# An attention output projection with its bias as a product on TensorE, row stores on GpSimd, and another order on SyncE and at the entry

## The reference

```python
x = x + attention(layernorm(x), ctx, ctx)        # ... @ Wo + bo
h = layernorm(x)
logits = h @ W_router.T + b_router               # 8 experts
w, idx = top_k(softmax(logits), 2)
x = x + sum(w * (h @ W_experts[idx].T + b_experts[idx]))
```

## Time and profile before

| | us |
|---|---|
| median of 3 runs | 2529.03 (2528.85 to 2530.27) |
| profiled execution, its own time | 2535.11 |
| its span | 2533.0 |

### The profile page before, as it was taken

How to read it: one execution, slowest core, us unless ns; L and a number is a source line. 1 busy time by engine, 2 the same in 40 slices (tenths; PEclk the granted TensorE clock), 3 DMA queues, 4 the chain that set the end, 5 groups by cost and what they waited for, 6 DMA issues and landing times. The chain is left out here.

```text
span 2533.0 us, 37104 instructions
## 1 busy us (share of the span) xinstructions
PE 2423.8 (96%) x13490; PEld 1286.3 (51%) x13490; DVE 2181.5 (86%) x1941; ACT 1836.9 (73%) x2150; POOL 424.0 (17%) x514
## 2 busy tenths in 40 slices
PE   8999779999999999999999999999999999869998
PEld 7878424444444444444444444444444447658776
DVE  4368569999999999999999999999999988876565
ACT  3123469999999998999999999999999854423343
POOL 2113200000000000000000000000000014336664
PEclk9999889999999999999999999999999999969999
DMA  7436781111152111115111112511111128734463
GB/s 268 155 127 219 199 202 27 26 27 30 26 121 56 27 26 31 26 30 138 36 26 31 26 27 50 126 26 31 26 26 47 31 97 307 250 108 143 133 220 118
DMA packets 145945, 230.90 MB, mean 91 GB/s; under 512 B 29126, under 2 KB 74662, under 8 KB 145004
## 3 DMA queue, kind: packets, MB, share of 16 engines
q1 hardware_dynamic: 123116, 176.93, 24.5%
q0 software_dynamic: 22016, 51.13, 6.4%
q10 hardware_dynamic: 640, 0.52, 0.1%
HBM read 154.75 MB, written 91.43 MB: 97 GB/s over the span
## 5 line engine op out<-in xcount | busy, mean ns | idle before, releaser
L1085 ACT ACTIVATE probs<-psum 128x1024 f32<-128x1024 f32 x1600 | 1513.4, 1034 | 138.5 <-PE psum L1239 131.6
L1239 PE MATMUL psum<-q_st,k_st 97*128 97x512 f32 x3200 | 923.7, 420 | 31.6 <-ACT probs L1085 18.9
L1239 PEld LDWEIGHTS psum<-q_st,k_st 97*128 97x128 f32 x3200 | 549.6, 189 | 609.5 <-ACT probs L1085 412.7
L1147 DVE TENSOR_TENSOR even_sums<-even_sums,probs 128x2048 f32<-128x2048 f32 x352 | 805.7, 2289 | 19.1 <-ACT probs L1085 19.1
L1260 PE MATMUL psum<-probs,v_st 128*32 128x512 f32 x6400 | 801.7, 602 | 0.0
L1147 DVE TENSOR_TENSOR odd_sums<-odd_sums,probs 128x2048 f32<-128x2048 f32 x320 | 731.3, 2285 | 1.0
L1260 PEld LDWEIGHTS psum<-probs,v_st 128*32 128x32 f32 x6400 | 152.5, 108 | 353.2 <-issue 273.6
L1990 PE MATMUL psum<-we_hi,wo 128*128 x624 | 218.8, 412 | 6.5 <-issue 6.2
L764 POOL DMA_DIRECT2D sum_scratch<-shared_rows x31 | 18.4, 593 | 1216.0 <-ACT shared_rows L1040 1216.0
L1847 ACT ACTIVATE wo<-psum 128x512 fp32r<-128x512 f32 x78 | 46.7, 598 | 136.5 <-PE psum L1976 115.5
L1990 PEld LDWEIGHTS psum<-we_hi,wo 128*128 128x128 f32 x624 | 119.0, 191 | 33.3 <-issue 7.7
(11 more groups left out here) (226 smaller groups left out, 2083.9 us busy)
## 6 DMA issues: line engine op xcount, KB each, us to landing
q_st<-qh_scratch SPq DMA_DIRECT2D x64, 256.0 KB
k_st<-kh_scratch SPq DMA_DIRECT2D x56, 192.0 KB, 3.8
token_rows<-rows SPq DMA_DIRECT2D x8, 1028.0 KB, 5.3
xn<-in_x SPq DMA_DIRECT2D x16, 512.0 KB, 6.7
qh_scratch<-o_hi SPq DMA_DIRECT2D x8, 1024.0 KB, 4.5
ql_scratch<-o_lo SPq DMA_DIRECT2D x8, 1024.0 KB, 7.1
q_st<-ql_scratch SPq DMA_DIRECT2D x32, 256.0 KB
token_rows<-in_x SPq DMA_DIRECT2D x1, 8192.0 KB, 36.3
```

The costliest lines, as they stand in the source:

```text
L1085: nc.scalar.activation(probs[:, p_slot(it, t), 2 * half:2 * half + 2, :], psum[:, 2 * slot:2 * slot + 2, :], ACT.Exp, scale=SCALE).then_in ...
L1147: nc.vector.tensor_tensor(into[:], a, probs[:, p_slot(it, t)], ALU.add).then_inc(added, 1)
L1239: mm = nc.tensor.matmul(psum[:, 2 * slot + h % 2, :], k_st[:, h, t * P:(t + 1) * P], q_st[:, b, h, :], start=True, stop=True)
```

## The change

The output bias is no longer added to x by GpSimd. A tensor `bo_pair` of 64 partitions holds the high part of the bias in rows 0 to 31 and the low part in rows 32 to 63 (512 columns), and beside it 128 columns that are zero but for ones in rows 0 and 32. `project_rows` begins with one product of the two, which puts the bias into psum; the 12 products add to it. The high part is copied by ScalarE and the low part computed by GpSimd during attention.

GpSimd issues `store_rows` and `store_mix` instead of SyncE. SyncE loads the attended rows at even i with the same condition on projection i + 1, ahead of the x load and the expert piece of that step, and loads x and pieces in another order at the start. At the entry ScalarE splits the first expert piece ahead of the last result; VectorE's preparation (`beside`) is spread behind the residuals of tiles 0 to 3; TensorE takes the router sums at step 2 behind project(2) instead of at step 0. One iota moves to `mix_experts`. Some small buffers are shared (`ex` with `below`, one `stats` for two).

```diff
@@ project_rows
+    bo, picks = g["bo_pair"][:, 0:g["D"]], g["bo_pair"][:, g["D"]:]
+    pe.matmul(psum[:, bank, :], picks, bo, start=True, stop=False)
     for t, (j, A, W) in enumerate(terms):
-        mm = pe.matmul(psum[:, bank, :], A[:, j, i % 2, :], W[:, j, :], start=t == 0, stop=t == len(terms) - 1)
+        mm = pe.matmul(psum[:, bank, :], A[:, j, i % 2, :], W[:, j, :], start=False, stop=t == len(terms) - 1)
@@ attention, gpsimd
+                    if it == 1:
+                        pool.wait_ge(bo_high_ready, 1)
+                        pool.tensor_tensor(bo_pair[DH:, 0:D], bo_raw[DH:, :], bo_pair[DH:, 0:D].bitcast(F32), ALU.subtract).then_inc(wo_lo_ready, 1)
@@ attention, scalar
+                        if it == 1 and n == NP // 3:
+                            act.wait_ge(small_in, 48)
+                            act.activation(bo_pair[:, 0:D], bo_raw[:], ACT.Copy).then_inc(bo_high_ready, 1)
@@ route_tokens, sync
-                for i in range(RING):
-                    load_x(i)
-                    load_piece(i)
+                load_x(0)
+                load_piece(0)
+                load_x(1)
+                load_x(2)
+                load_piece(1)
+                load_piece(2)
                 for i in range(NTL):
-                    if i % G4 == 2 and i > G4:
-                        store_rows(i // G4 - 1)
-                    if i % 2 and i // 2 + 2 < HEADS:
-                        sp.wait_ge(wo_mm, i + 1)
+                    if i % 2 == 0 and i // 2 + 2 < HEADS:
+                        sp.wait_ge(wo_mm, i + 2)
@@ route_tokens, gpsimd
+                for i in range(2, NTL + 1, 2):
+                    split_low(pool, i - 1, we_lo_pool)
+                    if i % G4 == 2 and i > G4:
+                        store_rows(i // G4 - 1)
                 store_rows(NGR - 1)
                 for q in range(NGR):
                     store_mix(q)
-                for i in range(NTL):
-                    with_bias(i)
-                    if i and i % 2 == 0:
-                        split_low(pool, i - 1, we_lo_pool)
-                split_low(pool, NTL - 1, we_lo_pool)
@@ route_tokens, scalar
+                split_high(0)
                 act.wait_ge(results["o_final"], LAST + 1)
...
-                    if i < NE * KT:
+                    if 0 < i < NE * KT:
                         split_high(i)
@@ route_tokens, vector
                 for i in range(STEPS):
                     if i < NTL:
                         residual(i)
+                        beside(i)
@@ route_tokens, tensor
-                    if i == 0:
+                    if i == 2:
                         pe.wait_ge(router_ready, 2)
@@ mix_experts, gpsimd
+                pool.iota(token[:], [[P, NTL]], base=1, channel_multiplier=1, allow_small_or_imprecise_dtypes=True).then_inc(counted, 1)
```

More of the change, by code:

```diff
@@ L916, in _ @@
                 fill_rows(pool, (0, HG // 2), rows_filled)
-                pool.wait_ge(rows_filled, K_PIECES)
+                pool.memset(bo_pair[:, D:].bitcast(F32), 0.0).then_inc(rows_filled, 1)
+                pool.wait_ge(rows_filled, K_PIECES + 1)
+                for r in (0, DH):
+                    pool.memset(bo_pair[r:r + 1, D:].bitcast(F32), 1.0).then_inc(rows_filled, 1)
+                pool.wait_ge(rows_filled, K_PIECES + 3)
                 pool.wait_ge(wo_hi_ready, 1)
@@ L1350, in route_tokens @@
     NTL, K, table, we_hi, we_lo, picked, before, mix = (h[n] for n in "NTL K table we_hi we_lo picked before mix".split())
-    lane, number, own, token, rows_stored = (h[n] for n in "lane number own token rows_stored".split())
+    lane, number, own, rows_stored = (h[n] for n in "lane number own rows_stored".split())
     mix_ready, mix_stored = h["mix_ready"], h["mix_stored"]
@@ L1377, in route_tokens @@
         of_shift = sb("of_shift", [P, G4, NE], F32)
-        stats = [sb(f"stats3{b}", [P, G4, 6], F32) for b in range(2)]
+        stats = sb("stats3", [P, G4, 6], F32)
         mv = sb("mv3", [P, G4, 2], F32)
@@ L1463, in _, with store_rows, store_mix @@
                         load_piece(i + 1)
+            @block.gpsimd
+            def _(pool):
+                def store_rows(q):
+                    pool.wait_ge(rows_ready, q + 1)
+                    pool.dma_start(table[q * G4 * P:(q + 1) * G4 * P, 0:MIX_AT].rearrange("(u p) c -> p u c", p=P),
+                                   rows[q % 2][:, :, 0:MIX_AT]).then_inc(rows_stored[q % 2], 16)
+                def store_mix(q):
+                    pool.wait_ge(mix_ready, q + 1)
+                    pool.dma_start(table[q * G4 * P:(q + 1) * G4 * P, MIX_AT:MIX_AT + K].rearrange("(u p) c -> p u c", p=P),
+                                   mix[:, q * G4:(q + 1) * G4, :]).then_inc(mix_stored, 16)
+                pool.wait_ge(small_in, 48)
+                pool.iota(number[:], [[1, NE]], base=0, channel_multiplier=0, allow_small_or_imprecise_dtypes=True).then_inc(counted, 1)
+                pool.iota(lane[:], [[1, P]], base=0, channel_multiplier=0, allow_small_or_imprecise_dtypes=True).then_inc(counted, 1)
+                pool.iota(own[:], [[1, 1]], base=0, channel_multiplier=1, allow_small_or_imprecise_dtypes=True).then_inc(counted, 1)
+                for i in range(2, NTL + 1, 2):
+                    split_low(pool, i - 1, we_lo_pool)
+                    if i % G4 == 2 and i > G4:
+                        store_rows(i // G4 - 1)
                 store_rows(NGR - 1)
@@ L1557, in residual @@
                     n[0] += 1
-                    dve.bn_stats(stats[q % 2][:, u, :], row).then_inc(chain, 1)
+                    dve.bn_stats(stats[:, u, :], row).then_inc(chain, 1)
                 def spread(q):
@@ L1703, in mix_experts @@
     NTL, K, NS, table, we_hi, we_lo, picked, before, mix = (h[n] for n in "NTL K NS table we_hi we_lo picked before mix".split())
[L1704 removed]
+    lane, own, mix_stored = (h[n] for n in "lane own mix_stored".split())
     wo = g["wo"]
```

92 lines of the change are left out of this document (40 added, 52 removed).

## The result

The changed kernel takes 2542.7 us (median of 6 runs, 2539.5 to 2547.9), the kernel before, beside it, 2530.2 (6 runs, 2528.9 to 2533.0). The ratio is 1.0044, with a 95% interval of 1.0034 to 1.0055: slower, where I had forecast 2521.6 and faster. The profiled execution took 2540.4 with a span of 2538.3.

A forecast was written before the change was run, and what follows sets the result against it. TensorE was taken to bound the routing loop, at 15.03 us a group. The terms -5.1 - 1.0 + 0.5 - 2.5 + 0.4 + 0.3 = -7.4 gave 2521.6 us from a median of 2529.03, range 2512.0 to 2528.5.

The forecast's parts named there:

- The entry: Start of the routing stage: p1 goes ahead of the router sum and the clock stays full, -5.1 us up to p7.
- The sign that no window from 2070 on would show a clock of 0.50: Check for the routing stage: TensorE's granted clock never at half of full from 2070 on.
- The bias product: One more TensorE product ahead of each projection: 0.50 us each, 31 times, +15.5 in the routing stage.
- the dear rival: Change of shape paid in full: each bias product costs 1.08 us, total 2539.6; chance 0.07.
- SyncE's new order: Routing loop: q_st loaded at even i ahead of x and piece; -1.0 us with bias products, +0.5 for remaining waits.
- all 13 us of loss go: Routing loop: TensorE loses no more time to late q_st, so a group costs 17.0 us, six 102.2 against 103.15.
- GpSimd's stores: Row and mix stores issued by GpSimd: 0.8 us each in the tail, bounds 0.5 and 2.0; later landing covered in the loop.
- The dear-stores rival: Tail: GpSimd's stores cost 2.0 us each, tail +8.3 instead of -2.5, total 2532.4; chance 0.05.
- The rest of the tail: End of the routing stage: ScalarE's 5.0 us wait for the last piece goes, rows_ready comes 3.4 us earlier against p31.
- VectorE: Without GpSimd's additions line 1583 falls from 1.21 to 0.19 us; worth nothing in the loop, counted in the tail.
- my conversion: The profiled execution, 2535.1 us, was 6 above its median, 2529.03; the forecast carried the trace difference over to the median.
- The waits for q_st only move: Routing loop: half of the 13 us loss stays beside the bias product, total 2528.1; chance 0.10.

The follow-up runs named there:

- f_sums_first: e_all3 with the sums of the router's weights put back at tile 0 instead of tile 2: 2522.8 us.
- e_qst_last: The changed kernel, but SyncE loads the attended rows at the end of even steps, behind the x load and the expert piece: 2528.5 us.
- e_both: The changed kernel with attended rows loaded behind x and piece, and row and mix stores issued by SyncE again: 2526.1 us.
- e_sp_stores: The changed kernel with all row and mix stores issued by SyncE again, the q_st load staying in front: 2528.5 us.
- b_qst_even: The kernel before, with only q_st loaded at even tiles ahead of x and piece: 2537.4 us.
- e_all3: e_both with the bias product padded with zeros to 128 rows: 2518.4 us, the fastest.
- f_pool_rows: e_all3 with only the row stores, and their final wait, moved to GpSimd: 2520.0 us.
- e_sp_mix: The changed kernel with only the eight small mix stores back on SyncE: 2535.8 us.
- b_pool_stores: The kernel before, with only the row and mix stores issued by GpSimd: 2538.7 us.
- f_pool_bias: e_both without the bias product, GpSimd adding the bias as in the kernel before: 2526.6 us.
- f_pool_mix: e_all3 with only the eight small mix stores moved to GpSimd: 2518.8 us.
- e_rows128: The changed kernel with the bias product padded with zeros from 64 to 128 rows: 2540.7 us.

## Why the prediction was wrong, step by step

**The entry was right:** -5.1 forecast, 4.96 measured (p7 at 2094.76). p1 starts 0.2 after the block opens, the clock stays at 1.00 up to p7, p4 starts 7.1 earlier where I had said 6. Half a microsecond of it is luck: the block opens at 2069.6 in this trace and at 2070.1 in that of before. f_sums_first shows the cause. The sign that no window from 2070 on would show a clock of 0.50 held at the entry and failed in the loop.

**The bias product was nearly right:** 0.50 forecast, 0.60 for one behind transposes and 0.54 in the mean of a group. The way in is 0.18, as at line 1672. The way out is 0.10 where I had put 0.08. The rest is the price of one product of the neighbours' shape, which I had taken as the pitch, 0.24, and which is 0.32. In the mean of a group the miss is 0.04, for 31 products 1.2 us. The Trainium skill, "TensorEngine Tiling (Array Packing)", section "Key Properties", says that a change of the mode drains TensorE; the trace agrees in kind, with 0.28 for the two changes around one product, far from the 0.84 of the dear rival.

**The step that failed is SyncE's new order.** I had written that the x load and the piece behind the moved wait "go out up to one tile later than now, but x(i+3) is used only after p(i+3)", and from that "all 13 us of loss go". For q_st this held: its waits are gone, and without the rest the six groups would have taken 103.2 (e_qst_last), where I had said 102.2. But I had followed x and not the piece. A piece is wanted by ScalarE, which rounds it ahead of its copy of the turned rows, and the router's product in TensorE's order wants the last copy of a group; the prediction doesn't speak of these copies. And I had counted when a load may be issued, not how much goes out with it: 2.0 MB in one burst, beside 1.0 MB of GpSimd's, and the piece that ScalarE stands for lands 8.6 us after its issue. Sized: +10.9 us in the loop with GpSimd's stores beside it (e_qst_last against the changed kernel) and +3.8 without (e_both against e_sp_stores), where I had +0.5. The same step in the kernel before alone gives +7.5 (b_qst_even).

**GpSimd's stores, the price of issuing was right, their end was not.** 0.74 to 0.77 each, forecast 0.8. But "the stage at 2222.0" took the last issue for the end. GpSimd's transfers land before the stage is left, and the mix stores behind the row store take 4.8 us for that: 11.63 from the last row store to the end against 6.73, +4.9 where I had +0.9 (7.7 from rows_ready to the end against 6.8). The dear-stores rival gave the right sign for the wrong reason (2.0 us an issue). I had also set the later landing in the loop (7.5 against 5.3 us) at nothing, covered by four psum banks. It is covered where TensorE holds the loop at 17.2 (e_qst_last against e_both); it is worth 7.1 together with the early q_st, 4.2 in the kernel before and 3.4 in e_all3 (f_pool_rows).
The Trainium skill, "DMA: Bandwidth & Descriptors", section "Specifications", gives the first byte as about 1 us by GpSimd's way and 0.6 by SyncE's, and its section "Issuing engine by pattern" gives simple stores to SyncE. No run here shows the first byte; the whole 1 MB of a row store lands 1.7 to 2.4 us later by GpSimd's way (medians, in four pairs of kernels that differ in who issues it; 0.7 in the fifth, e_sp_mix against e_sp_stores), so the traces agree on the side.

**The rest of the tail was right:** from p31 to the last row store 11.75 against 14.89, -3.14, where I had -3.4; the 5.0 us wait for the last piece is gone.

**VectorE.** I had priced line 1583 at 1.21 beside an addition. It does take that there (two of eight in the kernel before, six of eight in b_pool_stores), but in the kernel before it has a median of 0.19, as in the changed one, where it once takes 1.20 beside GpSimd's low part of a piece. So it says little on what leaving the additions is worth. The busy time of the windows above does: some 1.6 us in 16. I had given it nothing in the loop, since VectorE is not the bound. That reason was too short: f_pool_bias shows VectorE holding the q_st load through SyncE, and its six groups take 6.4 more than those of e_all3. In the tail, where I had counted it, the additions cost 2.3: 14.82 against 12.50 from the seventh router product to the last row store (f_pool_bias against e_both).

**The sum.** From the start of the trace to the end of the stage: -4.96 + 11.03 - 3.14 + 4.90 = +7.8, and 2.5 less in the expert stage, +5.3 in the span. Forecast was -7.4. Of these 12.7 us, 11.5 are the loop and 4.0 the end of the stage; entry and tail give 0.4, and the rest goes 3.2 the other way (-2.5 where I had +0.7). That last I can't put down to the change: behind the routing stage the kernel before takes 308.5 in its trace, but 305.2 and 306.6 in the two edits that leave that part as it was. The rest of the miss in the median, 21.1, is my conversion: the trace of before lay 4.9 above the median taken later, that of after 2.3 below its own, and the median of before had come out 1.2 lower the first time.

None of my rivals named what happened. "The waits for q_st only move" came nearest, but I had them move to q_st again, and the slower side was given to the product's price alone.

**What stays open.** Why the early q_st and the late stores together cost 10.9 in the loop, where the one alone costs 3.8 (e_sp_stores against e_both) and the other nothing. That one lateness uses up the spare of the other fits, and so does that GpSimd's row store is in flight with the burst; a kernel with a third buffer for the rows, which would tell them apart, wasn't tried. Why the same rows land later when GpSimd issues them is open as well. So is whether a later point in the step than the one in e_qst_last would let the loop go under 95.8.

## What to carry over

Before a load is moved ahead in a queue, follow each transfer behind it to the engine that uses it, and from there through that engine's fixed order to the bound engine; the one that is hurt here was three steps away. Count what is in flight together, by whichever engine it was issued, and when each of it lands, not when each may be issued. An engine that is never full can still hold the bound one, if a queue waits for it ahead of the load that the bound engine needs. And where GpSimd issues the last stores of a stage, the stage lasts until they have landed.

A product that differs in shape from its neighbours costs them the change twice; zeros that give it their shape halved its price, but that showed in the time only once the pieces and the stores were no longer late.

## What I had not expected of the hardware

- A stage is left 0.6 to 0.9 us after the last landing of GpSimd's transfers (landing 2231.4, end 2232.32 in the changed kernel; 2209.2 and 2209.76 in f_pool_mix; the same 0.9 in e_qst_last, b_pool_stores and e_rows128), though no semaphore of the mix stores is waited on there, while it is left before SyncE's have landed (last issue 2223.5, at least 3.6 to landing, end 2224.49).
- A mix store (4 KB) from GpSimd lands 2.2 to 2.5 us after its issue, alone or with others in a row (six of eight in f_pool_mix), but 4.9 to 5.2 when a row store of 1028 KB goes out beside it (the other two), and 4.5 to 5.0 behind one in the changed kernel. The same 1028 KB of rows land 7.5 us after issue from GpSimd and 5.3 from SyncE (medians of eight; over the kernels here 5.9 to 7.5 and 4.6 to 5.5).
- A product of 64 rows between products of 128 costs 0.28 us more than the same in 128 rows, 0.18 ahead of it and 0.10 behind (0.95 against 0.67 from transposes to projection).
